# Gathers of routed rows that wait for the stores of the tiles in use: a Perceiver block with a routed expert layer on one core

## The chip, the core and the metric

The kernel runs on 1 core of a Trainium2 chip. The metric is the device time of one execution in microseconds (us). Before the change three runs gave 951.27, 951.43 and 955.66 us, so the median is 951.43 us.

## What is computed

The input is x (16 x 64 x 512, so 1024 tokens of 512 numbers) and a context of 16 x 1601 x 512. Three blocks follow one another: cross attention to the context, attention with relative positions, and a feed-forward block, each fed by a layer norm and added to its input. The last part of the feed-forward block is the mixture of experts that the change is about, cut here to what matters:

```python
def moe(xn, ...):
    xt = xn.reshape(B * S, H)                                   # 1024 tokens x 512
    shared = silu(xt @ Wg_s) * (xt @ Wu_s) @ Wd_s
    probs = sigmoid(xt @ W_router + routing_bias)               # 7 experts
    scores, idx = top_k(probs, 2)                               # 2 picks for each token
    scores = scores / sum(scores)
    ...
    hmid = silu(g) * u                                          # each expert: 512 -> 512, gate and up
    combined = einsum('tei,eih,te->th', hmid, Wd_r, wts)        # down, weighted by the scores
    return shared + combined
```

All matrices are float32. The routing comes from the data. With the inputs of the reference the 2048 picks fall on the seven experts as 358, 321, 268, 382, 193, 246 and 280.

## The kernel before, in words

Each engine has its own program, written out by hand, and waits on semaphores. TensorE multiplies, VectorE (DVE) and ScalarE (ACT) empty its banks and form the operands, GpSimd (POOL) forms low parts of weights and issues the indirect DMAs, and SyncE (SP) issues the loads and the stores of the result.

Every large product is made of three: a float32 operand is split into a high and a low part (names with `_hi` and `_lo`), and TensorE adds low x high, high x low and high x high.

**Slots and tiles.** A pick is a pair of token and expert. The picks are sorted by expert into slots, and each expert's slots are rounded up to whole tiles of 128 rows. However the picks fall, `TILES` = 2048 / 128 + 6 = 22 tiles are enough, and 22 are always computed. With the counts above the experts take 3, 3, 3, 3, 2, 2 and 3 tiles, that is 19 in all, numbered 0 to 18. The tiles 19 to 21 hold no pick; they are computed with the weights of the last expert. DVE works out slots, tiles and gates in `allot()`: `first` is the number of tiles ahead of each expert, and its last entry (column `NR` = 7) is the number of tiles in use.

**Two scratch tensors in HBM.** `x_slots` and `y_slots` have 22 x 128 rows of 512 numbers. SP fills `x_slots` with zeros early (L427), from an SBUF tile `zeros`. When the slots are known, POOL scatters the tokens' rows into `x_slots` with 16 indirect DMAs (L1159, 8 groups of tokens x 2 picks). Then the tile loop runs.

**The tile loop.** For tile t, ACT loads 128 rows of `x_slots` (L1464); TensorE transposes them (L968); DVE splits them (L2088, L2093); TensorE makes gate and up (L958 to L960); ACT applies silu (L1468); DVE multiplies (L2100); TensorE transposes again (L991); ACT and DVE split (L1472, L2104); TensorE makes the down product (L958 to L960 again); ACT copies it out (L1478) and stores it to `y_slots` (L1480), counting on the semaphore `y_stored[0]` for even t and `y_stored[1]` for odd t. The down product of tile t comes after gate and up of tile t + 1, so the store of tile t is issued late in the step of tile t + 1.

**Weights.** Expert weights stand in a ring of three places of 24 KB per partition, at 0, 24 and 48 KB for the high parts (`ring_hi`) and at 72, 96 and 120 KB for the low parts. `PLACES = [0, 2, 1, 0, 2, 1, 0]` says which expert stands where; the last one stands in place 0. SP loads (L443) and POOL splits (L1171, L1173), the last splits long before the tile loop ends.

**The end.** After its splits POOL waits for all stores, and gathers the rows back:

```python
            for i in range(2):
                pool.wait_ge(y_stored[i], 16 * (TILES // 2))
```

Then come 16 indirect DMAs (L1180), one for each group k of 128 tokens and each of its 2 picks, into `picked[0]` to `picked[15]`. They count on five semaphores: groups 0 and 1, groups 2 and 3, groups 4 and 5, group 6, group 7. DVE, after its last tile instruction (L2104 of tile 21), adds them with their gates into `y`, two instructions for each group (L2123, L2124), and SP stores each group of `y` to the output (L448). The stretch of the program around it:

## Time and profile before

| | |
|---|---|
| median of three runs | 951.43 us |
| lowest and highest run | 951.27 and 955.66 us |
| span of the profiled execution, first to last instruction | 949.6 us |
| TensorE matmul busy in it | 844.9 us (89%) |
| DVE busy | 513.4 us (54%) |
| ACT busy | 308.5 us (32%) |
| GpSimd busy | 346.5 us (36%) |
| mean granted TensorE clock | 0.957 |

The profiled execution is known by its span; the time around that span is not in the trace. The median of the runs is 1.8 us above the span, and this difference is used to go from one to the other. Times below are counted from the span's start. Busy shares are averages over three blocks of different kinds; what happens after the tile loop is read from its own stretch.

### The profile page before, as it was taken

To read this page: it belongs to the slowest core of one execution; us is meant where nothing else is said; L and a number is where in the kernel's file an instruction comes from. 1 tells how busy PE (TensorE), PEld (TensorE's weight loads), DVE (VectorE), ACT (ScalarE), POOL (GpSimd) and SP (SyncE) were. 2 spreads that over 40 slices of the span, in tenths; PEclk is the share of its full clock that TensorE was granted. 3 is DMA by queue.
4 is the path that set the end of the run, shared out by engine and by line. 5 is a ranking of instruction groups with operands and counts; after the bars stand their busy time and mean duration, and the time that the engine had idled before them with its cause. 6 is when DMAs were issued, how large, how long until landed. Compare 5 with 4: busy or idle time off the path is not lost.

```text
span 949.6 us, 15932 instructions
## 1 busy us (share of the span) xinstructions
PE 844.9 (89%) x6032; PEld 624.6 (66%) x6049; DVE 513.4 (54%) x1110; ACT 308.5 (32%) x820; POOL 346.5 (36%) x172
## 2 busy tenths in 40 slices
PE   1899999998999998989889999799979999979950
PEld 1555555454587788868656766588858888868840
DVE  7766688566621255436757668854734343333304
ACT  2222333222503266621166567523301112111110
POOL 0000000002407235520053324632769999880015
PEclk9999999999979999999989999999989999999975
DMA  9757776555200210020640000030373555421027
GB/s 351 310 186 271 278 272 229 214 213 196 81 10 1 65 71 1 11 63 0 235 187 1 1 0 1 1 133 1 133 269 130 190 186 199 160 72 55 34 67 232
DMA packets 43865, 121.25 MB, mean 128 GB/s; under 512 B 3984, under 2 KB 8080, under 8 KB 37920
## 3 DMA queue, kind: packets, MB, share of 16 engines
q1 hardware_dynamic: 34912, 100.52, 28.6%
q10 hardware_dynamic: 6336, 11.54, 3.5%
q0 software_dynamic: 2560, 8.39, 2.7%
q8 instruction: 41, 0.67, 0.3%
q14 instruction: 16, 0.13, 0.0%
HBM read 102.05 MB, written 18.38 MB: 127 GB/s over the span
## 4 chain that ended last, share of the span: by engine, by line
PE 74%; DVE 8%; POOL 7%; DMA 5%; ACT 2%; issue 2%; SPq 0%; POOLq 0%; ACTq 0%; DVEq 0%
PE scores L474 10%; PE bank L501 8%; PE bank L958 6%; PE bank L960 6%; PE bank L959 6%; DMA nat<-in_ctx_keys 3%; PE bank L774 2%; POOL x_slots L1159 2%; PE bank L731 2%; PE bank L629 2%; PE bank L787 2%; PE bank L549 2%; PE bank L697 2%; DVE ctxT L1552 2%; PE bank L698 2%
## 5 line engine op out<-in xcount | busy, mean ns | idle before, releaser
L1552 DVE STREAM_TRANSPOSE ctxT<-nat 128x1024 f32<-128x1024 f32 (+3 forms) x120 | 120.7, 1067 | 6.2 <-DMA nat<-in_ctx_keys 6.0
L474 PE MATMUL scores<-ctxT,hn 32*64 32x384 f32 (+2 forms) x2048 | 93.4, 508 | 13.7 <-DVE ctxT L1552 13.6
L501 PE MATMUL bank<-nat,probT 128*64 128x512 f32 (+1 forms) x416 | 94.3, 598 | 0.0
L1052 POOL TENSOR_TENSOR wq_lo<-wq_raw,wq_hi 128x1024 fp32r<-128x1024 f32 x4 | 9.3, 2343 | 228.4 <-ACT wq_hi L1239 228.4
L474 PEld LDWEIGHTS scores<-ctxT,hn 32*64 32x64 f32 x2048 | 65.3, 133 | 38.2 <-issue 26.1
L1099 POOL TENSOR_TENSOR sp<-sp,s_inv 128x512 f32<-128x512 f32 x32 | 32.6, 1040 | 140.9 <-DVE s_inv L1857 140.9
L1173 POOL TENSOR_TENSOR ring_lo<-ring_raw,ring_hi 128x2048 fp32r<-128x2048 f32 x18 | 82.9, 4606 | 1.4
L958 PE MATMUL bank<-ring_hi,xg_lo 128*128 x176 | 73.3, 416 | 0.4 <-DVE y L2070 0.4
L960 PE MATMUL bank<-ring_hi,xg_hi 128*128 x176 | 69.6, 396 | 0.0
L959 PE MATMUL bank<-ring_lo,xg_hi 128*128 x176 | 69.3, 394 | 0.0
L1171 POOL TENSOR_TENSOR ring_hi<-ring_raw,cst 128x2048 fp32r<-128x2048 f32 x18 | 64.9, 3603 | 10.8 <-DMA ring_raw<-in_Wexp 10.8
L501 PEld LDWEIGHTS bank<-nat,probT 128*64 128x64 f32 (+1 forms) x416 | 28.0, 137 | 53.5 <-issue 53.4
L2104 DVE TENSOR_TENSOR rhm_lo<-bank,rhm_hi 128x512 fp32r<-128x512 f32 x22 | 15.2, 692 | 81.5 <-ACT rhm_hi L1472 81.5
L1390 ACT ACTIVATE sp<-bank,s_bias 128x128 f32<-128x128 f32 x128 | 45.0, 386 | 27.4 <-DVE s_bias L1852 27.4
L1478 ACT COPY hn<-bank 128x512 f32<-128x512 f32 x22 | 12.9, 586 | 117.4 <-PE bank L960 117.4
L1180 POOL DMA_INDIRECT picked<-y_slots,slots x16 | 16.4, 1026 | 73.6 <-DMA y_slots<-hn 69.1
L1206 ACT ACTIVATE prob<-scores,nmax 128x512 f32<-128x512 f32 x24 | 16.2, 683 | 76.9 <-DVE nmax L1547 76.9
L2088 DVE TENSOR_SCALAR xg_hi<-bank,vec 128x128 fp32r<-128x128 f32 x88 | 24.8, 344 | 30.1 <-PE bank L968 29.8
L1543 DVE TENSOR_REDUCE mx<-scores 128x2 f32<-128x832 f32 x8 | 8.2, 1025 | 56.1 <-PE scores L474 56.1
L960 PEld LDWEIGHTS bank<-ring_hi,xg_hi 128*128 128x128 f32 x176 | 33.4, 190 | 7.7
L958 PEld LDWEIGHTS bank<-ring_hi,xg_lo 128*128 128x128 f32 x176 | 33.7, 191 | 6.3 <-issue 0.7
L959 PEld LDWEIGHTS bank<-ring_lo,xg_hi 128*128 128x128 f32 x176 | 33.7, 191 | 5.9
(277 smaller groups left out, 2010.4 us busy)
## 6 DMA issues: line engine op xcount, KB each, us to landing
nat<-in_ctx_keys SPq DMA_DIRECT2D x46, 1024.0 KB, 7.5
ring_raw<-in_Wexp SPq DMA_DIRECT2D x21, 1024.0 KB, 9.2
x_slots<-zeros SPq DMA_DIRECT2D x1, 5632.0 KB, 26.2
hn<-x_slots ACTq DMA_DIRECT2D x22, 256.0 KB, 3.1
y_slots<-hn ACTq DMA_DIRECT2D x22, 256.0 KB, 2.1
w_raw<-in_Wexp SPq DMA_DIRECT2D x3, 1024.0 KB, 11.2
nat<-in_ctx_keys SPq DMA_DIRECT2D x16, 130.0 KB
wq_raw<-in_Wq SPq DMA_DIRECT2D x1, 2048.0 KB, 7.6
```

The lines of the kernel that those rows point to most:

```text
L474: last = nc.tensor.matmul(scores4[64 * b:64 * b + 64, i, 0:KEYS_IN[i]], q4[rows_i, j, 64 * b:64 * b + 64], ctxT[rows_i, b, j, 0:KEYS_IN[i] ...
L501: last = nc.tensor.matmul(bank[7][64 * b:64 * b + 64, :], probT[0:n, j, 64 * b:64 * b + 64], nat[k % 2][0:n, b, j, :], start=j == 0, stop= ...
L549: nc.tensor.matmul(bank[4 + m % 4][:], lo, hh, start=c == 0, stop=False)
L958: nc.tensor.matmul(b[:], x_lo[:, c, :], hi, start=c == 0, stop=False)
L959: nc.tensor.matmul(b[:], x_hi[:, c, :], lo, start=False, stop=False)
L960: last = nc.tensor.matmul(b[:], x_hi[:, c, :], hi, start=False, stop=c == HC - 1)
L1099: nc.gpsimd.tensor_tensor(sp_[par][:, 4 * c:4 * c + 4, :], sp_[par][:, 4 * c:4 * c + 4, :], s_inv[par][:, 4 * c:4 * c + 4].unsqueeze(2).br ...
L1171: nc.gpsimd.tensor_tensor(ring_hi[at], ring_raw[at], zero, ALU.add).then_inc(split_hi, 1)
L1173: last = nc.gpsimd.tensor_tensor(ring_lo[at], ring_raw[at], ring_hi.bitcast(F32)[at], ALU.subtract)
L1390: last = nc.scalar.activation(sp_[par][:, h, :], score_bank(k, c)[:, n * P:(n + 1) * P], ACT.Exp, bias=s_bias[par][:, h:h + 1], scale=SELF ...
L1552: dve.transpose(dst, src).then_inc(columns_ready, 1)
L2088: last = dve.tensor_scalar(xg_hi[par][:, c, :], columns[c], weights[c], None, ALU.mult)
```

## The change

POOL no longer waits for all 22 stores before it gathers, but for the number of stores of each parity that the tiles in use make. DVE works these two numbers out with three small instructions in `allot()` (compare the tile numbers with the count of tiles in use, times 16, and add up even and odd tiles), and signals them on `slots_ready` as the fifth count. POOL reads them into registers after its splits, waits for `y_stored[0]` and `y_stored[1]` to reach them, passes a semaphore of its own (`used_stored`), and gathers. It waits for all 22 stores at its end.

`picked` moves from 0 to 32 KB to 24 to 56 KB per partition, that is out of the weight place 0 and into the places 1 and 2. SP fills `y_slots` with zeros too, in a second DMA right behind the first (22 x 128 rows, 5632 KB each), and POOL and DVE wait for both fills where they waited for one.

```diff
--- before.py
+++ after.py
@@ -160,7 +160,9 @@
         gates = [sbuf(ctx, f"gates{i}", [P, NT]) for i in range(2)]
         slots = sbuf(ctx, "slots", [P, NT, 2], U32)
         tile_expert = sbuf(ctx, "tile_expert", [P, 2, TILES], I32)
+        used_stored = sem("used_stored")
         expert_begins = sbuf(ctx, "expert_begins", [P, NE], I32)
+        stored_need = sbuf(ctx, "stored_need", [P, 2], I32)
         rbias_sb = sbuf(ctx, "rbias_sb", [P, NR])
         wrout_sb = sbuf(ctx, "wrout_sb", [P, HC, NR])
         a_max, a_bias, a_sum, a_inv = ([sbuf(ctx, f"{n}{i}", [P, NH]) for i in range(2)]
@@ -269,6 +271,8 @@
         r_fill = place(68, "r_fill", [P, NE, NE])
         r_tile = place(68.25, "r_tile", [P, 2, TILES])
         r_slot = place(68.5, "r_slot", [P, NT, 2])
+        r_used = place(68.75, "r_used", [P, TILES])
+        r_need = place(69, "r_need", [P, 2])
 
         ring_hi = place(0, "ring_hi", [P, RING3, 3, HC, D], F32R)
         ring_raw = place(72, "ring_raw", [P, RING3, 3, HC, D])
@@ -280,7 +284,7 @@
         rhm_hi = place(174, "rhm_hi", [P, HC, P], F32R)
         rhm_lo = place(148, "rhm_lo", [P, HC, P], F32R)
         yo = hn[2:4]
-        picked = [place(2 * i, f"picked{i}", [P, D]) for i in range(2 * NT)]
+        picked = [place(24 + 2 * i, f"picked{i}", [P, D]) for i in range(2 * NT)]
 
         pos_dram = nc.dram_tensor("pos_dram", (BATCH, SEQ * PADDED * NH), F32).ap()
 
@@ -424,8 +428,9 @@
                 sp.dma_start(w_raw[m][:], matrix(m, 0)).then_inc(raw_loaded, 16)
 
             sp.wait_ge(cleared, 3)
-            sp.dma_start(x_slots.rearrange("(t p) d -> p t d", p=P),
-                         zeros[:].unsqueeze(1).broadcast_to([P, TILES, D])).then_inc(slots_zeroed, 16)
+            for rows_of in (x_slots, y_slots):
+                sp.dma_start(rows_of.rearrange("(t p) d -> p t d", p=P),
+                             zeros[:].unsqueeze(1).broadcast_to([P, TILES, D])).then_inc(slots_zeroed, 16)
 
             for e in range(NR):
                 if e == 0:
@@ -1152,7 +1157,7 @@
                     columns_low(2 + 2 * j)
                     columns_low(3 + 2 * j)
 
-            pool.wait_ge(slots_zeroed, 16)
+            pool.wait_ge(slots_zeroed, 2 * 16)
             pool.wait_ge(slots_ready, 1)
             for k in range(NT):
                 for i in range(2):
@@ -1173,12 +1178,19 @@
                     last = nc.gpsimd.tensor_tensor(ring_lo[at], ring_raw[at], ring_hi.bitcast(F32)[at], ALU.subtract)
                 last.then_inc(split_ready, 1)
 
+            pool.wait_ge(slots_ready, 5)
+            need = [pool.value_load(stored_need[0:1, i:i + 1], min_val=16 * (TOK // P), max_val=16 * (TILES // 2))
+                    for i in range(2)]
             for i in range(2):
-                pool.wait_ge(y_stored[i], 16 * (TILES // 2))
+                pool.wait_ge(y_stored[i], need[i])
+            pool.sem_inc(used_stored, 1)
+            pool.wait_ge(used_stored, 1)
             for k in range(NT):
                 for i in range(2):
                     nc.gpsimd.indirect_dma_start(picked[2 * k + i][:], None, y_slots,
                                                  bass.IndirectOffsetOnAxis(slots[:, k, i:i + 1], 0)).then_inc(picked_loaded[picked_part(k)[0]], 16)
+            for i in range(2):
+                pool.wait_ge(y_stored[i], 16 * (TILES // 2))
 
         def query_out(copy, f, sem_done):
             copy(q4[:, 4 * f:4 * f + 4, :].rearrange("p j q -> p (j q)"), bank[QUERY_BANK[f]][:]).then_inc(sem_done, 1)
@@ -2035,7 +2047,10 @@
                 chain(dve.reciprocal(r_key[:], r_key[:]))
                 chain.mark(dve.tensor_tensor(gates[0][:], gates[0][:], r_key[:], ALU.mult))
                 dve.tensor_tensor(gates[1][:], gates[1][:], r_key[:], ALU.mult).then_inc(slots_ready, 1)
-                dve.wait_ge(slots_ready, 4)
+                chain(dve.tensor_scalar(r_used[:], cst[:, C_TILE:C_TILE + TILES], first[:, NR:NE], 16.0, ALU.is_lt, ALU.mult))
+                chain(dve.tensor_reduce(r_need[:], r_used[:].rearrange("p (t a) -> p a t", a=2), AX, ALU.add))
+                dve.tensor_copy(stored_need[:], r_need[:]).then_inc(slots_ready, 1)
+                dve.wait_ge(slots_ready, 5)
                 chain.wait()
 
             expert_stats(NT - 1, NT)
@@ -2045,7 +2060,7 @@
             expert_scale(NT // 2, NT)
             dve.tensor_copy(below_bf[:], cst[:, C_BELOW:C_BELOW + P]).then_inc(consts_cast, 1)
             dve.memset(ones_bf[:], 1.0).then_inc(consts_cast, 1)
-            dve.wait_ge(slots_zeroed, 16)
+            dve.wait_ge(slots_zeroed, 2 * 16)
             for j in range(NJ):
                 dve.wait_ge(silu_ready, j + 1)
                 if j >= 2:
```

Below are rows of the programs as they are built, in the order in which each engine issues them.

On POOL, the end of its program, before. The rows are the last two splits and the gathers; DMA stands for an indirect DMA:

```order
L1171 TENSOR_TENSOR ring_hi<-ring_raw,cst 128x2048 [waits routed_loaded2]
L1173 TENSOR_TENSOR ring_lo<-ring_raw,ring_hi 128x2048 [waits split_hi]
L1180 DMA picked0<-y_slots,slots 128x512 [waits y_stored1,y_stored0]
L1180 DMA picked1<-y_slots,slots 128x512
...
L1180 DMA picked15<-y_slots,slots 128x512
L122 UNCONDITIONAL_BRANCH
```

The same place after:

```order
L1176 TENSOR_TENSOR ring_hi<-ring_raw,cst 128x2048 [waits routed_loaded2]
L1178 TENSOR_TENSOR ring_lo<-ring_raw,ring_hi 128x2048 [waits split_hi]
L1182 TENSOR_LOAD stored_need [waits slots_ready]
L1182 ISA x2
L1182 TENSOR_LOAD stored_need
L1182 ISA x2
L1190 DMA picked0<-y_slots,slots 128x512 [waits y_stored0,y_stored1,used_stored]
L1190 DMA picked1<-y_slots,slots 128x512
...
L1190 DMA picked15<-y_slots,slots 128x512
L122 UNCONDITIONAL_BRANCH [waits y_stored1,y_stored0]
```

Two register loads have come between the splits and the first gather, the gathers stand in the same order, and the wait for all stores has gone behind the last of them.

On SP, the place where the scratch is filled, before (the four loads ahead of it are weights; L443 is the first load into the ring):

```order
L424 DMA w_raw32<-in_Wexp 128x4x512
L427 DMA x_slots<-zeros 128x22x512 [waits cleared]
L443 DMA ring_raw<-in_Wexp 128x4x512 [waits wo_full]
```

And after:

```order
L428 DMA w_raw32<-in_Wexp 128x4x512
L432 DMA x_slots<-zeros 128x22x512 [waits cleared]
L432 DMA y_slots<-zeros 128x22x512
L448 DMA ring_raw<-in_Wexp 128x4x512 [waits wo_full]
```

The second fill stands behind the first and ahead of the ring's loads; it waits for nothing of its own.

On DVE, the end of `allot()` and the shared expert's next step after the change (`gates` are the scores, `hm` the shared expert's hidden values):

```order
L2048 TENSOR_TENSOR gates0<-gates0,r_key 128x8 [waits dve_step]
L2049 TENSOR_TENSOR gates1<-gates1,r_key 128x8
L2050 TENSOR_SCALAR r_used<-cst,r_first 128x22
L2051 TENSOR_REDUCE r_need<-r_used 128x2 [waits dve_step]
L2052 CAST stored_need<-r_need 128x2 [waits dve_step]
L2068 TENSOR_TENSOR hm0<-act_g0,bank5 128x512 [waits silu_ready,hlo_ready,dve_step,slots_ready]
```

Three small instructions have come in ahead of that step. The rest of DVE's program, and TensorE's and ACT's, keep their order.

## Rows read from the trace of the kernel before

**Rows 1.** The page's first line.
```profile
span 949.6 us, 15932 instructions
```

**Rows 2.** Waits, 890 to 950 us: total us, times, longest us.
```profile
DVE y L2123 <- DMA picked<-y_slots,slots: 23.1, 5, 15.7
```

**Rows 3.** Timeline, ACT's queue: start us, us, line, operation.
```profile
892.75 0.36 ACTq L1480 DMA_DIRECT2D y_slots<-hn  x1
...
917.37 0.34 ACTq L1480 DMA_DIRECT2D y_slots<-hn  x1
```

**Rows 4.** Timeline, POOL, at the gathers.
```profile
920.25 0.98 POOL L1180 DMA_INDIRECT picked<-y_slots,slots  x1 [69.05 <-DMA y_slots<-hn]
...
927.80 1.39 POOL L1180 DMA_INDIRECT picked<-y_slots,slots  x1 [0.30 <-issue]
...
940.02 1.21 POOL L1180 DMA_INDIRECT picked<-y_slots,slots  x1 [0.30 <-issue]
```

**Rows 5.** Timeline, DVE, its last tile instruction and the additions.
```profile
911.27 0.69 DVE L2104 TENSOR_TENSOR rhm_lo<-bank,rhm_hi 128x512 fp32r<-128x512 f32 x1 [3.66 <-ACT rhm_hi L1472]
927.62 0.75 DVE L2123 SCALAR_TENSOR_TENSOR y<-picked,gates,y 128x512 f32<-128x512 f32 x1 [15.65 <-DMA picked<-y_slots,slots]
...
929.07 0.75 DVE L2123 SCALAR_TENSOR_TENSOR y<-picked,gates,y 128x512 f32<-128x512 f32 x1
...
934.64 0.77 DVE L2123 SCALAR_TENSOR_TENSOR y<-picked,gates,y 128x512 f32<-128x512 f32 x1 [4.03 <-DMA picked<-y_slots,slots]
...
942.59 0.75 DVE L2123 SCALAR_TENSOR_TENSOR y<-picked,gates,y 128x512 f32<-128x512 f32 x1 [0.73 <-DMA picked<-y_slots,slots]
...
945.57 0.75 DVE L2123 SCALAR_TENSOR_TENSOR y<-picked,gates,y 128x512 f32<-128x512 f32 x1 [1.44 <-DMA picked<-y_slots,slots]
946.36 0.75 DVE L2124 SCALAR_TENSOR_TENSOR y<-picked,gates,y 128x512 f32<-128x512 f32 x1
```

**Rows 6.** Timeline, DVE, first and last split of rows for the last expert.
```profile
851.30 1.12 DVE L2093 SCALAR_TENSOR_TENSOR xg_lo<-bank,vec,xg_hi 128x128 fp32r<-128x128 f32 x4 [7.99 <-POOL ring_lo L1173]
...
896.69 1.13 DVE L2093 SCALAR_TENSOR_TENSOR xg_lo<-bank,vec,xg_hi 128x128 fp32r<-128x128 f32 x4
```

**Rows 7.** The chain that ended last, in order of time.
```profile
917.37 2.05 DMA y_slots<-hn
919.46 0.79 issue
```

**Rows 8.** The page's DMA issues: count, KB each, median us to landing.
```profile
x_slots<-zeros SPq DMA_DIRECT2D x1, 5632.0 KB, 26.2
```

**Rows 9.** Timeline, SP's queue, around the fill.
```profile
460.74 2.77 SPq L427 DMA_DIRECT2D x_slots<-zeros  x1
624.01 197.79 SPq L443 DMA_DIRECT2D ring_raw<-in_Wexp  x21
```

**Rows 10.** Timeline, DVE, the shared expert's hidden values and the end of `allot()`.
```profile
631.40 0.63 DVE L2053 TENSOR_TENSOR hm<-act_g,bank 128x512 f32<-128x512 f32 x1
...
669.18 0.16 DVE L2037 TENSOR_TENSOR gates<-gates,r_key 128x8 f32<-128x8 f32 x1
...
673.97 0.69 DVE L2053 TENSOR_TENSOR hm<-act_g,bank 128x512 f32<-128x512 f32 x1 [2.53 <-ACT act_g L1448]
```

**Rows 11.** DMA queues, 900 to 950 us: packets, MB, share of 16 engines.
```profile
q0 software_dynamic: 1280, 4.20, 29.6%
q1 hardware_dynamic: 1152, 2.10, 11.0%
```

**Rows 12.** Timeline at the scatters, a DVE instruction and the scatter beside it.
```profile
682.19 2.28 DVE L2077 TENSOR_TENSOR ring_lo<-ring_raw,ring_hi 128x2048 fp32r<-128x2048 f32 x1
...
682.81 2.49 POOL L1159 DMA_INDIRECT x_slots<-xx,slots  x1 [0.30 <-issue]
```

**Rows 13.** Windows: us, then busy us (count) by engine, TensorE clock, DMA share, GB/s.
```profile
460.70:487.00 26.30, 21.70 (x100) 15.04 (x101) 20.32 (x74) 15.48 (x49) 4.24 (x5) 0.91 0.98 372
487.00:513.00 26.00, 25.52 (x178) 18.59 (x182) 16.21 (x34) 14.69 (x54) 14.06 (x7) 0.96 0.01 2
```

## The prediction

> **What bounds the kernel now.** I read the waits of the last 60 us first, then the timelines of the four engines that take part there, then the chain that ended last. The last multiplication feeds the store of tile 21, which ACT issues at 917.37 [rows 3]. It lands 2.05 us later and POOL starts 0.79 us after that [rows 7], at 920.25, after 69.05 us without work [rows 4]. POOL then issues 16 gathers one after another, the last one at 940.02, some 1.3 us apiece. DVE had finished its tile work at 911.27 + 0.69 = 911.96 and stood idle for 15.65 us; after that it waited three more times in the rows shown, the last until 945.57, and ended at 946.36 + 0.75 = 947.11 [rows 5]. In all DVE waited 23.1 us for gathered rows [rows 2]. So from 917 to 947 us nothing but the gathers sets the time: the end is their start plus 26.9 us, and the span ends 2.5 us after DVE, at 949.6 [rows 1], with the last output store.
>
> **Which tiles are in use.** The change pays only if the last tile in use is earlier than tile 21. The routing counts of the inputs give 19 tiles, the last one number 18. The trace bears out where the last expert begins: at 851.30 DVE waited 7.99 us for POOL's last split, the one wait on a new expert's weights so late. The last such step, at 896.69, is that of tile 21 [rows 6]; between the two lie four more steps, so 851.30 is tile 16, and the expert's 280 picks fill tiles 16, 17 and 18. There are two stores between the two of [rows 3] (tiles 19 and 20), so the one at 892.75 is that of tile 18. Even tiles 0 to 18 are 10 stores and odd tiles 1 to 17 are 9.
>
> **The gathers' new start.** The store of tile 18 is issued at 892.75. With the same landing and start as for tile 21, POOL begins at 892.75 + 2.05 + 0.79 = 895.6, which is 24.7 us earlier. The register loads of the two counts stand before the wait, and POOL is idle for 69 us there [rows 4], so they are hidden by about 40 us. The semaphore that POOL raises and waits for itself isn't in the trace; between nothing and the 0.30 us that POOL leaves between two gathers I take 0.1 and leave it out of the sum, since what follows does not hang on it.
>
> **What DVE does then.** It can't use the rows before 911.96, its last tile instruction, which comes from TensorE and has nothing to do with the gathers. By the old distances the rows of groups 0 and 1 are there at 927.62 - 24.7 = 903.0, those of 2 and 3 at 910.0, those of group 6 at 917.9 and of group 7 at 920.9 [rows 5]. DVE's additions come in pairs 929.07 - 927.62 = 1.45 us apart, and a pair takes 947.11 - 945.57 = 1.54. Starting at 912.0 it comes to group 6 at 920.7 and to group 7 at 922.1, behind the rows by 2.7 and 1.2 us. So it adds without a pause and ends at 912.0 + 7 x 1.45 + 1.54 = 923.7. Before it ended at 947.1: **23.4 us less**. The gathers' wait is gone, and what is late next is DVE itself, by a narrow 1.2 us over the last gather. TensorE's last product (before 917) and tile 21's store (landing at 919.4) end earlier than that, so POOL's wait for all stores at its end costs nothing. The output stores leave as DVE ends each group, 1.45 us apart; eight of them are 11.0% of 50 us, 0.7 us of all 16 engines each [rows 11], so they keep up and the last 2.5 us stay.
>
> **The second fill.** The first one goes out at 460.74 and lands 26.2 us later, at 487 [rows 8, 9]. It used the DMA engines wholly (share 0.98); in the next 26 us they are all but idle, 0.01 [rows 13]. The second fill takes those, to 513. SP's next load goes out at 624.01 [rows 9], and DVE's first instruction behind the fill's wait is at 631.40 [rows 10]. That is a cover of 111 us; without it the cost would be 26.2. The weights' loads stand ahead of the fills in the queue. What other work there is at 487 to 513 can be slowed only by traffic that it doesn't issue itself. As a bound: TensorE was busy 21.7 of 26.3 us in the first fill and 25.5 of 26.0 after it [rows 13]. If all of that were the fill's doing, the second would cost up to 3.8 us. Self-attention is just starting in the first window, with one step's work and no neighbour to fill in, so I take 0.
>
> **DVE's three small instructions.** They are like the small ones beside them, 0.16 us each and a little for the step's semaphore, 0.2 apiece [rows 10]: 0.6 us, and they delay the hidden values that follow at once. The next of these waits 2.53 us for ACT, until 673.97 [rows 10], so the delay is swallowed there. The scatters are released earlier, by the slots, and don't see it. 0 on the path, 0.6 if that slack were gone. The place of `picked` changes nothing that is timed: places 1 and 2 have no reader once tile 15 is done, place 0 still has.
>
> **Sum.** 23.4 less than the span of 949.6 is 926.2; the median of the runs stands 1.8 above the span, which gives **928.0 us**.
>
> **A rule weighed against the trace.** At 927.80 a gather that began beside DVE's addition took 1.39 us, against 0.98 for the first one [rows 4], and at 682.81 a scatter beside a DVE instruction of 2.28 us, both of whose inputs are in SBUF, took 2.49 [rows 12]; that one was stopped for all of it. The four last gathers now fall between 911 and 917 and so beside unbroken additions. The Trainium skill, "SBUF — State Buffer", Who interferes with whom, says that a DVE instruction with two SBUF inputs contends with a GpSimd instruction that reads SBUF, and that the loser is blocked for the whole instruction. By the scatter's row each of the four would be held for a whole addition, 0.75 us: 3.0 us, while 0.6 of such delay is in the old times already (1.39 - 0.98, and 1.21 - 0.98 in the last one) [rows 4]; group 7 would then be there at 920.9 + 3.0 - 0.6 = 923.3, 1.2 us after DVE comes to it, and the time would be 929.2. By the gather's own row, 0.4 each, group 7 is there at 920.9 + 1.6 - 0.6 = 921.9, before DVE comes to it at 922.1, and the sum stands. I take the gather's row.
>
> **Rivals.**
> 1. The gathers stay the bound. They now run beside tile work, tile stores and output stores. For it: the slack is only 1.2 us, and the sixteen gathers are 29.6% of 50 us, 0.9 us of all engines each [rows 11], at one in 1.3 us; with an output store of 0.7 in every 1.45 us that is more than 1. Against: only four or five gathers meet output stores, and in the old run ten did. Price, at the worst row for every gather (1.39 + 0.30): the last starts 15 x 1.69 = 25.4 after 895.6, at 921.0, lands 5.55 later (940.02 to 945.57), at 926.5; then 1.54 and 2.5 and 1.8: 932.4. It decides from 1.2 us of delay on.
> 2. The second fill slows self-attention by the 3.8 us above: 931.8.
> 3. The wait is not shortened, because the count of tiles in use comes out as 22: no gain, and up to 0.6 us of small instructions, 951.4 to 952.0. The last expert's start at tile 16 speaks against it.
> 4. The other side, slower: something on the path at 487 to 513 waits until the second fill has drained. If it stood still for the fill's whole 26.2 us, the time would be 928.0 + 26.2 = 954.2, slower than before by 2.8; the point from which it decides the sign is a stop of 23.4 us, and it takes 28.2, more than the fill is long, to be slower by over half a per cent. In the first fill, just as dense, DVE was busy for 20.3 of 26.3 us [rows 13], so nothing stood still.
>
> **How the numbers follow.** Forecast as reasoned 0.74, between 926 and 929.5; rival 1 0.12, 929 to 932.4; rival 2 0.05; rival 3 0.03; rival 4 0.02 (mostly with its time a little under the bound of half a per cent); something unthought that eats between 5 and 20 us of the gain 0.04. The range is 925.5 to 932.5: the low end is the DVE-bound end less what three runs can differ (lowest and highest before are 4.4 apart, so 2.5), since no gather can bring the end before DVE's 923.7; the high end takes in rivals 1 and 2. About 0.87 lies inside. Half a per cent, 4.8 us, is about what a measurement can tell from no change: faster 0.95, same 0.035, slower 0.015.
>
> **What would show each step.** In the changed kernel's timeline the first gather should start at 895 to 896, about 2.8 us after the fourth-last tile store. DVE should start adding within 0.1 us of its last tile instruction and have no wait for gathered rows, or under 0.5 us at groups 6 and 7. SP should issue two fills by 466, the second landing near 513, with TensorE's busy time in 487 to 513 as now. The tile loop should end where it did, at 912 for DVE and 917 for TensorE. The prediction is wrong if DVE waits for the last groups by more than 2 us, if the tile loop starts later than before, or if the first gather still follows tile 21.

## The result, and the profile after

The changed kernel took 938.09 us (median of four runs, 932.90 to 938.98), the kernel before 951.35 us (the three runs already told and a fourth, 949.93 to 955.66): a ratio of 0.9839, interval 0.9807 to 0.9872. It is faster, by 1.6%, but the time lies 10.1 us above the forecast of 928.0 and 5.6 us above the top of the range. The profiled execution took 932.9 us and had a span of 931.0, 5.0 to 6.2 us less than the spans of the other three; it alone has a trace. The page's first line:

```profile
span 931.0 us, 15960 instructions
```

The first gathers do what was predicted. ACT's queue and ACT (the store of tile 18, the silu of tile 21's gate, the copy of tile 20's down product), in the timeline of the changed kernel:

```profile
888.14 0.36 ACTq L1492 DMA_DIRECT2D y_slots<-hn  x1
...
908.08 0.60 ACT L1480 ACTIVATE rhm<-bank 128x512 f32<-128x512 f32 x1 [10.08 <-remote]
...
913.90 0.59 ACT L1490 COPY hn<-bank 128x512 f32<-128x512 f32 x1 [5.22 <-remote]
```

POOL in the same timeline, its first and its last gather:

```profile
891.09 0.98 POOL L1190 DMA_INDIRECT picked<-y_slots,slots  x1 [44.12 <-POOLq L1186]
...
909.90 0.95 POOL L1190 DMA_INDIRECT picked<-y_slots,slots  x1 [0.30 <-issue]
```

The first gather starts 2.95 us after the store of tile 18; the prediction had 2.84. Both come about 4.6 us earlier than [rows 3] let expect, since in this execution the whole tile loop ran that much earlier, well before any gather (set 2 below shows where that comes from). DVE in the same timeline, from its multiplication of tile 20 on:

```profile
893.68 0.69 DVE L2115 TENSOR_TENSOR rhm<-rhm,bank 128x512 f32<-128x512 f32 x1 [0.45 <-PE bank L965]
...
898.04 0.69 DVE L2119 TENSOR_TENSOR rhm_lo<-bank,rhm_hi 128x512 fp32r<-128x512 f32 x1 [3.67 <-issue]
913.78 0.69 DVE L2115 TENSOR_TENSOR rhm<-rhm,bank 128x512 f32<-128x512 f32 x1 [15.05 <-remote]
916.29 0.69 DVE L2119 TENSOR_TENSOR rhm_lo<-bank,rhm_hi 128x512 fp32r<-128x512 f32 x1 [1.83 <-ACT rhm_hi L1484]
916.90 0.74 DVE L2138 SCALAR_TENSOR_TENSOR y<-picked,gates,y 128x512 f32<-128x512 f32 x1
...
927.04 0.75 DVE L2138 SCALAR_TENSOR_TENSOR y<-picked,gates,y 128x512 f32<-128x512 f32 x1
```

The waits for gathered rows of [rows 2] and [rows 5] are gone: DVE adds without a pause, 10.14 us from the first pair to the last, and starts 0.08 us before its last tile instruction ends (916.29 + 0.69 = 916.98), so right behind it. A new wait of 15.05 us stands ahead of tile 21's multiplication. It needs the product "up" of tile 21, and the releaser is given as "remote": no engine's instruction in the trace ended there. The views of the waits (890 to 950 us) and of TensorE's timeline say what had been done by then. The waits:

```profile
DVE rhm L2115 <- remote: 15.0, 1, 15.0
ACT rhm L1480 <- remote: 10.1, 1, 10.1
```

TensorE, the last matmul of the gate of tile 21, of its up, of the down of tile 20, and then its next work:

```profile
899.19 0.39 PE L965 MATMUL bank<-ring_hi,xg_hi 128*128 x1
...
901.91 0.39 PE L965 MATMUL bank<-ring_hi,xg_hi 128*128 x1
...
904.63 0.39 PE L965 MATMUL bank<-ring_hi,rhm_hi 128*128 x1
914.52 1.11 PE L996 MATMUL bank<-cst,rhm 128*128 128x128 f32 x4 [9.51 <-DVE rhm L2115]
```

TensorE ended the gate at 899.58, the up at 902.30 and the down at 905.02. ACT took the gate at 908.08, DVE the up at 913.78, ACT the down at 913.90: 8.5, 11.5 and 8.9 us after the last matmul of each. In `e1_again` below, DVE starts within 0.1 us of the same product's end. So the work was finished and the word of it came late. The gathers are in the air just then: the last is issued by 910.85, and the last record of a landing of theirs is at 913.71. The trace's semaphore records show the rise itself as late (908.06, 913.75 and 913.88). Only TensorE's word is late: ACT's silu ends at 908.68, and DVE's wait for it (L2114) is over at 908.74, as the chain that ended last has it:

```profile
908.72 0.02 DVEq L2114
908.74 5.02 another core or an unknown queue
913.75 0.02 issue
913.78 0.70 DVE rhm L2115
```

The trace also has 379 records of semaphore rises fewer than that of the kernel before (5034 against 5413; `e1_again` below, the same kernel, has 5431), missing at the scatters (671 to 690 us) and at the gathers (896 to 908). I call this **the stop** below.

The window that holds it, with the columns of [rows 13]:

```profile
893.00:917.40 24.40, 13.41 (x60) 10.59 (x59) 3.41 (x6) 2.94 (x5) 13.58 (x15) 0.79 0.63 192
```

TensorE is busy for 13.4 of 24.4 us. Its mean granted clock is 0.79 there, but that is no cause: the last matmuls before the stop are 0.23 us apart, as those of the other profiles are, and the clock is 1.00 from 893 to 905 us and 0.61 from 905 to 914.5, so it fell once the engine had nothing to do.

The fills (SP's queue, and the landing of the second), and the window after the first fill:

```profile
462.21 2.63 SPq L432 DMA_DIRECT2D x_slots<-zeros  x1
464.88 16.09 SPq L432 DMA_DIRECT2D y_slots<-zeros  x1
...
625.45 1.48 SPq L448 DMA_DIRECT2D ring_raw<-in_Wexp  x3
```

```profile
y_slots<-zeros SPq DMA_DIRECT2D x1, 5632.0 KB, 38.5
```

```profile
487.00:513.00 26.00, 25.71 (x158) 19.46 (x157) 15.37 (x33) 15.37 (x50) 15.55 (x9) 0.93 0.57 222
```

SP was held 16.09 us by the issue of the second fill, against 2.63 by the first, yet its next load leaves at 625.45, against 624.01 before [rows 9]. The second fill lands 38.5 us after its issue, at 503.4, about 14 us behind the first and not 26. TensorE is busy for 25.71 of 26.00 us in the window in which it runs, against 25.52 before [rows 13].

### The profile page after: what moved, and what is told of

Its sections match the earlier page's. It is cut to its first block, busy times and chain, and to the rows that moved or that the text cites. A ratio compares the mean times of both kernels' runs of the same rounds, so it can differ in the third digit from the quotient of the medians.

```text
span 931.0 us, 15960 instructions
## 1 busy us (share of the span) xinstructions
PE 847.3 (91%) x6048; PEld 624.6 (67%) x6049; DVE 512.5 (55%) x1113; ACT 308.4 (33%) x820; POOL 341.8 (37%) x172
## 4 chain that ended last, share of the span: by engine, by line
PE 73%; DVE 8%; POOL 8%; DMA 5%; issue 3%; ACT 2%; another core or an unknown queue 1%; SPq 0%; POOLq 0%; DVEq 0%; ACTq 0%
PE scores L479 10%; PE bank L506 8%; PE bank L963 4%; PE bank L965 4%; PE bank L964 4%; DMA nat<-in_ctx_keys 3%; POOL ring_lo L1178 3%; PE bank L779 2%; POOL ring_hi L1176 2%; PE bank L736 2%; PE bank L792 2%; PE bank L554 2%; PE bank L634 2%; PE bank L702 2%; DVE ctxT L1564 2%
## 5 line engine op out<-in xcount | busy, mean ns | idle before, releaser
L479 PE MATMUL scores<-ctxT,hn 32*64 32x385 f32 (+2 forms) x2048 | 94.9, 512 | 13.3 <-DVE ctxT L1564 13.2
L479 PEld LDWEIGHTS scores<-ctxT,hn 32*64 32x64 f32 x2048 | 65.8, 134 | 38.6 <-issue 27.5
L1555 DVE TENSOR_REDUCE mx<-scores 128x2 f32<-128x832 f32 x8 | 8.2, 1024 | 56.3 <-PE scores L479 56.3
L2103 DVE TENSOR_SCALAR xg_hi<-bank,vec 128x128 fp32r<-128x128 f32 x88 | 24.8, 345 | 24.7 <-PE bank L973 24.4
L963 PE MATMUL bank<-ring_hi,rhm_lo 128*128 x88 | 35.1, 399 | 1.5 <-DVE rhm_lo L2119 1.5
## 6 DMA issues: line engine op xcount, KB each, us to landing
y_slots<-zeros SPq DMA_DIRECT2D x1, 5632.0 KB, 38.5
```

The costliest lines, as they stand in the source:

```text
L479: last = nc.tensor.matmul(scores4[64 * b:64 * b + 64, i, 0:KEYS_IN[i]], q4[rows_i, j, 64 * b:64 * b + 64], ctxT[rows_i, b, j, 0:KEYS_IN[i] ...
L963: nc.tensor.matmul(b[:], x_lo[:, c, :], hi, start=c == 0, stop=False)
L2103: last = dve.tensor_scalar(xg_hi[par][:, c, :], columns[c], weights[c], None, ALU.mult)
```

## The experiments

A set is a group of kernels run one after the other on one chip, together with the kernel before; ratios are to the kernel before of the same set. The result above is set 1; sets 2 to 9 follow, 8 on the chip of 7 and 9 on that of 5. "The stop" is the late word from TensorE in the profile above.

**Set 2: the changed kernel again, and with single parts changed.** `e1_again` is the changed kernel as it is.

> The changed kernel once more. In its first profile the gates product of tile 21 ended on TensorE near 899 us, but its semaphore reached ScalarE at 908.06, and that of the up product reached VectorE at 913.75 instead of near 902; 915 us is also about where the last gathered rows landed. Theory G (the gathers hold something back that TensorE's signals or the engines' code need): the same stop of 9 to 15 us in tile 20 or 21 is seen again, ending near the landing of the last gather, and the span is 930 to 938. Theory L (a single mishap of one execution): no stop, VectorE's last tile instruction ends at 912 and the span is 926 to 927.

929.42 us (927.87 to 931.96), ratio 0.9782 (0.9723 to 0.9840), span 927.4. The stop isn't there. DVE in its timeline:

```profile
899.52 0.69 DVE L2115 TENSOR_TENSOR rhm<-rhm,bank 128x512 f32<-128x512 f32 x1 [0.45 <-PE bank L965]
...
908.18 0.69 DVE L2115 TENSOR_TENSOR rhm<-rhm,bank 128x512 f32<-128x512 f32 x1 [3.61 <-PE bank L965]
912.52 0.69 DVE L2119 TENSOR_TENSOR rhm_lo<-bank,rhm_hi 128x512 fp32r<-128x512 f32 x1 [3.65 <-ACT rhm_hi L1484]
913.12 0.74 DVE L2138 SCALAR_TENSOR_TENSOR y<-picked,gates,y 128x512 f32<-128x512 f32 x1
...
923.27 0.75 DVE L2138 SCALAR_TENSOR_TENSOR y<-picked,gates,y 128x512 f32<-128x512 f32 x1
924.05 0.75 DVE L2139 SCALAR_TENSOR_TENSOR y<-picked,gates,y 128x512 f32<-128x512 f32 x1
```

And POOL, the first gather and the last three:

```profile
896.93 0.98 POOL L1190 DMA_INDIRECT picked<-y_slots,slots  x1 [44.26 <-POOLq L1186]
...
913.24 1.45 POOL L1190 DMA_INDIRECT picked<-y_slots,slots  x1 [0.30 <-issue]
914.99 1.14 POOL L1190 DMA_INDIRECT picked<-y_slots,slots  x1 [0.30 <-issue]
916.44 1.15 POOL L1190 DMA_INDIRECT picked<-y_slots,slots  x1 [0.30 <-issue]
```

This sizes the stop. From the multiplication of tile 20 to the last split it is 912.52 - 899.52 = 13.00 us here and 916.29 - 893.68 = 22.61 in set 1: **9.6 us late**. From the split to group 7 it is 10.75 us in both.

The profiled execution of set 1 isn't 9.6 us longer than this one, though, but 3.6 (spans of 931.0 and 927.4), since its tile 20 came 5.8 us earlier (893.68 against 899.52). The like late signals at POOL's scatters go with that. DVE in set 1's timeline, an addition of the shared expert and its next two long splits of weights, and POOL, the scatter that was held longest and the last one:

```profile
682.34 0.69 DVE L2085 TENSOR_TENSOR y<-bank,y 128x512 f32<-128x512 f32 x1 [4.06 <-remote]
682.94 2.28 DVE L2092 TENSOR_TENSOR ring_lo<-ring_raw,ring_hi 128x2048 fp32r<-128x2048 f32 x1
...
689.28 2.28 DVE L2092 TENSOR_TENSOR ring_lo<-ring_raw,ring_hi 128x2048 fp32r<-128x2048 f32 x1
```

```profile
684.16 1.90 POOL L1164 DMA_INDIRECT x_slots<-xx,slots  x1 [0.30 <-issue]
...
688.89 0.96 POOL L1164 DMA_INDIRECT x_slots<-xx,slots  x1 [0.30 <-issue]
```

And POOL in `e1_again`, the last of the three scatters that were held there and the last of all:

```profile
687.25 2.50 POOL L1164 DMA_INDIRECT x_slots<-xx,slots  x1 [0.31 <-issue]
...
692.58 0.96 POOL L1164 DMA_INDIRECT x_slots<-xx,slots  x1 [0.30 <-issue]
```

The scatters begin at 668.8 and 668.9 us. In `e1_again`, as in [rows 12], three of them stand beside DVE's splits and take 2.4 to 2.5 us each; in set 1 DVE came late, one scatter was held, and the last ended 3.7 us earlier. The store of tile 0 was issued at 715.9 us there, against 722.2. So in the traced execution the stop cost 9.6 us at tile 21, and late signals at the scatters had given most of 5.8 us ahead of it. The median of set 1 less 9.6 is 928.5, close to this set's 929.42, but the two belong to different executions: 938 is the time of three that have no trace. It would fit if they had the late tile 21 without the early tile loop (927.4 + 9.6 = 937.0, an estimate, against spans of 936.0 to 937.2); that is not shown.

`e2_late` keeps everything but the early start:

```diff
                 pool.wait_ge(y_stored[i], need[i])
+            for i in range(2):
+                pool.wait_ge(y_stored[i], 16 * (TILES // 2))
             pool.sem_inc(used_stored, 1)
```

> All of the change but the early start: POOL waits for the counts of the tiles in use and then for all 22 stores before it gathers. It keeps the second fill, the three small instructions, the register loads and the new place of the gathered rows. If the prediction's zeros for these hold, 951.4 us, within 1. If the second fill or the small instructions are what is missing from the gain, 955 to 962, with the loss seen before 893 us. The stop in tile 21 should be gone in every theory in which early gathers cause it.

953.76 us (ten runs, 949.05 to 955.35), ratio 1.0034 (1.0006 to 1.0063); the profiled execution had a span of 949.6, the same as before's. The median is 2.4 us above the 951.4 expected. So the second fill, the small instructions, the new place and the register loads give back at most 0.6%, and the profile shows none of it. The early start, all that parts this kernel from `e1_again`, is worth 953.76 - 929.42 = 24.3 us.

`e3_place96` puts the gathered rows in a third place:

```diff
-        picked = [place(24 + 2 * i, f"picked{i}", [P, D]) for i in range(2 * NT)]
+        picked = [place(96 + 2 * i, f"picked{i}", [P, D]) for i in range(2 * NT)]
```

> The change with the gathered rows at 96 to 128 KB of each partition instead of 24 to 56 KB. If the stop comes from where the gathers write (near the weights at 0 to 24 KB that TensorE reads), it goes or moves and the time is 928. If it comes from the gathers as such, the time is that of the changed kernel, 933 to 939, and the stop is there.

927.09 us, ratio 0.9748 (0.9683 to 0.9813). No stop in it, but none in the kernel beside it either, so it says only that this place costs nothing.

`e4_plain_sp` drops POOL's gathers; SP copies as many bytes with plain DMAs, the first 2048 rows of the scratch instead of the routed ones, so the routed gather is left out:

```diff
+            sp.wait_ge(used_stored, 1)
+            for k in range(NT):
+                for i in range(2):
+                    sp.dma_start(picked[2 * k + i][:], y_slots[(2 * k + i) * P:(2 * k + i + 1) * P, :]).then_inc(
+                        picked_loaded[picked_part(k)[0]], 16)
...
-                    nc.gpsimd.indirect_dma_start(picked[2 * k + i][:], None, y_slots,
-                                                 bass.IndirectOffsetOnAxis(slots[:, k, i:i + 1], 0)).then_inc(picked_loaded[picked_part(k)[0]], 16)
```

> The change with the 16 gathers replaced by 16 plain DMAs of the same size from SyncE, started by the same counts of stores; they copy rows 0 to 2047 of the scratch and not the routed rows, so the output differs. If the stop comes from indirect DMAs that GpSimd issues, it is gone: VectorE ends its tile work at 912, adds without a pause, and the time is 928. If the load on the DMA engines itself does it, the stop stays, maybe shorter, since plain loads of 256 KB take about 2 us each: 930 to 936.

928.65 us, ratio 0.9774 (0.9710 to 0.9838). SP's queue issued all sixteen by 903.7:

```profile
895.12 8.61 SPq L454 DMA_DIRECT2D picked<-y_slots  x16
```

DVE added from 912.07, a pair every 1.45 us as in `e1_again`. Faster transfers win nothing: DVE is the bound, not the gathers.

**Set 3: load, order and the other bound.** `e5_again` is the changed kernel once more.

> The changed kernel a third time. Theory L (the stop in tile 21 that the first profile showed is a rare event, or belongs to one chip): no stop in the profile, 925.5 to 932.5 us, and a ratio of 0.975 to 0.98. Theory G (the gathers cause it each time with some chance): among six executions at least one is 5 us or more above the fastest, and the profile shows the stop again with a chance of one half.

928.87 us (six runs, 925.54 to 931.15), ratio 0.9767 (0.9736 to 0.9798), no stop. `e6_double` puts 16 more gathers, thrown away, ahead of the real ones:

```diff
+            for i in range(2):
+                pool.wait_ge(y_stored[i], 16 * 8)
+            for k in range(NT):
+                for i in range(2):
+                    nc.gpsimd.indirect_dma_start(picked[2 * k + i][:], None, x_slots,
+                                                 bass.IndirectOffsetOnAxis(slots[:, k, i:i + 1], 0)).then_inc(scattered, 16)
+            pool.wait_ge(scattered, 16 * 4 * NT)
```

> The change with 16 more gathers of the same size, thrown away, that begin when the stores of tiles 0 to 15 have landed (near 867 us) and end ahead of the true ones, so that three more tiles are computed beside gathers. If gathers hold back TensorE's signals (theory G), stops of 5 us or more now show in tiles 17 to 21 too, and the time is 933 or more. If they don't (theory L), the tile loop keeps its 9.1 us for each tile and the time is 926 to 931; the added gathers are hidden, since they end by about 891, before the store of tile 18 lands.

927.73 us, ratio 0.9764 (0.9731 to 0.9798). POOL's first gather of each kind:

```profile
868.03 0.98 POOL L1188 DMA_INDIRECT picked<-x_slots,slots  x1 [16.48 <-DMA y_slots<-hn]
...
895.30 0.94 POOL L1197 DMA_INDIRECT picked<-y_slots,slots  x1 [7.53 <-POOLq L1193]
```

32 gathers beside the tile loop delay no tile, in a set whose unchanged kernel has no stop either. So gathers do not slow the loop by their number or their traffic alone; what stopped set 1 takes something more.

`e7_between` lets DVE add groups 0 and 1 before the last tile's multiplication:

```diff
+            add_rows(range(2))
             routed_mult(TILES - 1)
             hidden_split(TILES - 1)
...
+            add_rows(range(2, NT))
```

> The change with VectorE's additions for groups 0 and 1 moved into its idle time of 3.6 us between its last instructions for tile 20 and tile 21. The end of the changed kernel is set by 8 pairs of additions behind tile 21; two of them, 2 x 1.45 = 2.9 us, now lie in idle time if their rows are there at 904, as they should be (7.4 us after the first gather). If VectorE's additions set the end, 2.9 us less than the changed kernel of the same call. If the gathers do, no change, and VectorE waits for the last groups.

927.09 us, ratio 0.9748 (0.9718 to 0.9778). DVE now waits for the rows of group 0 and for those of group 7:

```profile
906.09 0.75 DVE L2137 SCALAR_TENSOR_TENSOR y<-picked,gates,y 128x512 f32<-128x512 f32 x1 [1.06 <-DMA picked<-y_slots,slots]
...
922.62 0.75 DVE L2137 SCALAR_TENSOR_TENSOR y<-picked,gates,y 128x512 f32<-128x512 f32 x1 [1.65 <-DMA picked<-y_slots,slots]
```

Its first gather started at 897.38, so group 7's rows were there 25.2 us after it. In `e1_again` that would be 922.1, and DVE came to them at 923.27: a slack of 1.1 us, against the 1.2 predicted. Taking 2.9 us of additions off DVE's end can therefore win only 1.1 to 1.8 us, and the two medians differ by 1.8 with intervals that overlap.

`e8_tile20` starts the gathers one even tile later, after tile 20's store:

```diff
                 pool.wait_ge(y_stored[i], need[i])
+            pool.wait_ge(y_stored[0], 16 * 11)
             pool.sem_inc(used_stored, 1)
```

> The change, but the gathers also wait for the store of tile 20, the first after tile 18 of the even ones. They then start 2.8 us after 910.3, at 913.1, and the last rows land 25.3 us later at 938.4, or 22.6 us later as in the first profile of the changed kernel, at 935.7; with 1.5 for the last pair, 2.5 to the span's end and 1.8 around it the time is 941.5 to 944.2. So 13 to 16 us of the gain come from the two last tiles, and the first of the three would be worth little, since VectorE is the bound from there on. If the start of the gathers mattered one for one, it would be 17.5 us over the changed kernel, 945 to 947.

944.67 us (941.97 to 944.98), ratio 0.9929 (0.9900 to 0.9957). POOL, its first gather:

```profile
914.53 0.98 POOL L1191 DMA_INDIRECT picked<-y_slots,slots  x1 [61.41 <-POOLq L1187]
```

DVE, the first addition and that of group 7:

```profile
922.44 0.75 DVE L2139 SCALAR_TENSOR_TENSOR y<-picked,gates,y 128x512 f32<-128x512 f32 x1 [9.21 <-DMA picked<-y_slots,slots]
...
939.02 0.75 DVE L2139 SCALAR_TENSOR_TENSOR y<-picked,gates,y 128x512 f32<-128x512 f32 x1 [0.42 <-DMA picked<-y_slots,slots]
```

Here the gathers bound the end again. They start 17.6 us later than in `e1_again`, and the additions of group 7 are 15.8 us later (939.02 - 923.27): between the two lie 1.8 us of slack, by this reading. The time is 0.5 us over what was expected at most; the gathers started at 914.53 where 913.1 had been reckoned.

**Sets 4 to 6: to meet the stop again.** Set 4 is `e9_again` (the changed kernel) and `e10_plain_sp` (as `e4_plain_sp`):

> The changed kernel a fourth time, to see whether the stop before tile 21's last steps comes back. In the first set all four executions stood at 933 to 939; in two later sets ten stood at 925.5 to 932.0, without a stop in either profile. Theory C (it belongs to the chip of that set): on another chip again 926 to 932 without a stop. Theory G (chance, from the gathers): a stop in the profile, or single executions at 933 or more.

> Plain DMAs of SyncE in place of the gathers once more (rows 0 to 2047 of the scratch, so the output differs), beside the changed kernel. If the changed kernel of this call shows the stop and this one doesn't, indirect DMAs from GpSimd cause it; if both show it, the load of the DMA engines does; if neither does, both are 926 to 931 and nothing is told but that the stop is rare.

928.63 us, ratio 0.9763 (0.9732 to 0.9794), and 929.17 us, ratio 0.9783 (0.9756 to 0.9811). No stop in either. Set 5 is `e11_again`:

> The changed kernel in a fifth set. Theory C (the stop belongs to the chip or the moment of the first set): no stop, 926 to 932, unless the set falls on that chip, where all executions would stand at 933 to 939 again. Theory G (the gathers bring it by chance): a stop in the profile or single executions at 933 or more.

929.31 us, ratio 0.9775 (0.9740 to 0.9810), no stop. Set 6 is `e12_aftermult`, which moves the additions of groups 0 and 1 one step on from where `e7_between` has them:

```diff
             routed_mult(TILES - 1)
+            add_rows(range(2))
             hidden_split(TILES - 1)
...
+            add_rows(range(2, NT))
```

> As the kernel with two groups' additions ahead of tile 21's last steps, but they stand one step later, between VectorE's multiplication and its split of tile 21, where it has 3.65 us without work (908.87 to 912.52 in the repeated run of the changed kernel). In the earlier version VectorE waited for group 0 until 906.1 and tile 21's multiplication came 0.5 us late; here the rows are there and nothing is late, and the two pairs fill 2.9 us. The last group's rows then set the end: 25.2 us after the first gather, against 26.3 us in the changed kernel, so about 1.1 us less than that: 927.5 to 928, within what can be told from the changed kernel. If the additions were still the bound, it would be 2.9 less.

932.12 us (930.33 to 935.02), ratio 0.9866 (0.9841 to 0.9891), with the kernel before at 944.76 in that set. **The stop is back.** Its waits (890 to 950 us):

```profile
DVE rhm L2115 <- remote: 15.4, 1, 15.4
ACT rhm L1480 <- remote: 13.9, 1, 13.9
```

And ACT and DVE in its timeline:

```profile
911.87 0.60 ACT L1480 ACTIVATE rhm<-bank 128x512 f32<-128x512 f32 x1 [13.91 <-remote]
914.07 0.69 DVE L2115 TENSOR_TENSOR rhm<-rhm,bank 128x512 f32<-128x512 f32 x1 [15.38 <-remote]
```

The tile before was at 893.64, as in set 1. The gate product ended at 899.5 and ACT saw it 12.3 us later; the up product ended at 902.3, and DVE saw it 11.8 us later. Again records of semaphore rises are missing at the scatters and at the gathers (5016 are there). As in set 1 only one scatter was held (2.03 us), and the store of tile 0 went out at 716.2. Ratios tell the two cases apart as the traces do: 0.9839 and 0.9866 with the stop, 0.9736 to 0.9787 for the unchanged code without it. The time alone hardly does, 932.1 us against 927.6 to 930.1, because the kernel before was faster too, 944.76 against 950.2 to 952.3 in the other sets from 2 on; late signals at its scatters, with nothing to delay at its end, would do that, but no trace of it was kept in this set. The additions that this kernel moves stand behind the late multiplication, so they haven't made it late; by its trace up to there this is the changed kernel, in a set that has the stop.

**Sets 7 to 9: the chip, or the indirect DMAs?** Set 7 is `e13_plain_sp` (as `e4_plain_sp`):

> Plain DMAs of SyncE in place of the 16 gathers (rows 0 to 2047 of the scratch, so the output differs). The two profiles with the stop also show TensorE's signals 6 us late beside GpSimd's scatters near 682 us, which this kernel keeps. So each set tells by the scatters whether it is of the kind that shows the stop. Theory I (indirect DMAs issued by GpSimd hold TensorE's signals back on some chips): in such a set the scatters show late signals, and tile 21 doesn't, VectorE ends its tile work at its usual time. Theory D (any dense load of the DMA engines does it there): tile 21 shows late signals of 5 us or more as well. In a set without late signals at the scatters both say 926 to 931 and nothing is told.

928.08 us, ratio 0.9744 (0.9712 to 0.9776). DVE in its timeline, an addition of the shared expert while POOL's scatters run, and then tile 21:

```profile
681.46 0.69 DVE L2086 TENSOR_TENSOR y<-bank,y 128x512 f32<-128x512 f32 x1 [3.31 <-PE bank L1028]
...
908.32 0.69 DVE L2116 TENSOR_TENSOR rhm<-rhm,bank 128x512 f32<-128x512 f32 x1 [3.60 <-PE bank L970]
```

At the scatters TensorE's signals come up to 2.9 us late in this execution (5.9 in set 1 and 6.2 in `e12_aftermult`, where the like of the 3.31 us wait shown is 4.1 and 4.2 us; it is 2.03 in the kernel before), and records are missing there again (5285 are there); at tile 21, beside plain DMAs, nothing is late: 3.60 us is the usual wait. Set 8, on the same chip, is `e14_plain_sp` and `e15_again`:

> Plain DMAs in place of the gathers again (other rows, so the output differs), beside the changed kernel on the same chip. In a set whose scatters show late signals of TensorE: theory I, no late signal in tile 21 here, 925 to 930 us, and 4 to 10 us less than the changed kernel. Theory D, the stop here too and the same time. In a set without them both kernels are within 2 us.

> The changed kernel beside e14. In a set whose scatters show late signals: the stop in tile 21 and 932 to 939 us, a gain of 13 to 18 us instead of 22. In a set without them: 926 to 932, no stop.

926.77 us, ratio 0.9721 (0.9690 to 0.9753), and 927.57 us, ratio 0.9736 (0.9701 to 0.9772). No late signal in either, at scatters or gathers: the chip alone doesn't decide. Set 9, on the chip of set 5, is `e16_again`, `e17_between` and `e18_plain_sp`:

> The changed kernel with the next two on one chip. e13 and e14 were the same kernel on the same chip, one with late signals at the scatters and one without, so it is not the chip as such. If it belongs to a stretch of time or to a program as loaded, about two of seven profiles of this kind show it: then 932 to 939 with the stop, otherwise 926 to 932.

> The kernel with two groups' additions ahead of tile 21's last steps, beside the changed kernel: 0.7 to 2 us less than e16 if neither shows the stop, since the last gathered rows are the bound at 25.2 us after the first gather. With the stop, VectorE is late anyway and the time is 930 or more.

> Plain DMAs in place of the gathers (other rows, so the output differs). Theory I: even if the scatters show late signals, tile 21 shows none and the time is 926 to 930. Theory D: with them, a stop of 5 us or more in tile 21.

930.09 us, ratio 0.9787 (0.9754 to 0.9820); 930.55 us, ratio 0.9773 (0.9735 to 0.9812); 927.11 us, ratio 0.9733 (0.9693 to 0.9772). No stop in any of the three. Adding two groups ahead of the last tile is not shown to beat the changed kernel on either chip, and the plain DMAs are 0.5% ahead here, with intervals that overlap, and level in the other sets.

## Why the prediction was right in its steps and wrong in its time

- **The gathers' new start: right.** 2.95 us after the store of tile 18 in set 1 and in `e1_again`, 2.84 predicted; the difference is the 0.1 us set aside for the semaphore. In [rows 4] the like start was 27.5 us after that same store.
- **DVE the next bound, by a narrow margin: right.** In `e1_again` DVE adds from 913.12 in pairs of 1.45 us and ends at 924.80; predicted 912.0, 1.45 and 923.7. The 1.1 us between are the tile loop's, which ended that much later in this execution. The slack over group 7 is 1.1 us by `e7_between` and 1.8 by `e8_tile20`, predicted 1.2. The rule that was weighed went as taken: the gathers that met additions in `e1_again` took 0.2 to 0.5 us more and not 0.75, and DVE did not wait for group 7. `e4_plain_sp` shows that no faster transfer would help, `e8_tile20` what the kernel is when they do bound it. Rival 1 (the gathers stay the bound) falls with that.
- **The second fill at nothing: right as far as the runs tell.** TensorE's busy time beside it is that of before, DVE and SP are covered as said, and `e2_late` has before's span. Its runs stand above the kernel before by an interval of 0.06 to 0.63%, so rival 2's 3.8 us (0.4%) isn't excluded by the times; the profile speaks against it. Its length was wrong: the prediction gave it the first fill's 26.2 us, to 513, and it was over at 503.4; the first one's time also holds the weights' loads ahead of it in the queue (four of 1024 KB in the window from 460 us). SP's queue was held for 16.09 us, which the prediction had not reckoned, and 144 us without work behind it hid that.
- **The small instructions at nothing: right.** They took 0.9 us rather than 0.6 and shortened the wait behind them, from 2.53 [rows 10] to 1.8 us.
- **"The tile loop should end where it did": this step failed.** The prediction took the tile loop's last tile as a thing that "has nothing to do with the gathers", put DVE's start at 912.0 from it, and had no term and no rival for what the gathers would do to TensorE's side of it. In set 1's traced execution TensorE's finished products were made known 8.5 to 11.5 us late while the gathers ran, and the last tile ended 9.6 us late, reckoned from tile 20: DVE began to add at 916.90 instead of 912.0, although tile 20 had been early. The three executions that set the median lie 5 to 6 us higher still, with no trace to tell it apart. The cause stays open. Before the change the gathers began when no product was awaited, so the same thing would have cost nothing there. The case "something unthought that eats between 5 and 20 us" was this one; it had 0.04.
- **Where the stop is absent, the whole number held.** The unchanged code, timed in six more sets, took 927.57, 928.63, 928.87, 929.31, 929.42 and 930.09 us: each within 2.1 us of 928.0 and inside the range.

What is shown of the stop and what not: it was met with POOL's indirect gathers in two of the twelve profiles in which they run beside the last tiles; it was met at POOL's scatters in the same two and, weaker, in `e13_plain_sp`; in the five profiles in which plain DMAs took the gathers' part, one of them with the late signals at its scatters, tile 21 was never late. It seems to stay with a set (the three further executions of set 1, by their times of 937.8 to 939.0, had it too), changes from set to set on one chip, and isn't brought by twice as many gathers. That the indirect DMAs delay TensorE's signals fits all of this, but it rests on coincidence in three profiles; no experiment could turn it on. Another coincidence points the same way: in set 1 the last late rises come as the landings end, at the gathers (last landing recorded at 913.71, rises at 913.75 and 913.88) and at the scatters (691.61; 691.56 and 691.69). What makes one set have it and another not stays open, and so does whether the missing records are its cause, its effect or only the trace's loss: every timed run here was recorded like the profiled ones, so none tells whether the recording itself takes part.

## What to carry to other kernels

When a wait is shortened so that a transfer runs beside the end of another stage, that stage's end becomes a term of the sum: look for what the transfer shares with it, and give a case of its own to the stage ending late. When a narrow slack is what follows, the next bound lies just behind it; here a further 2.9 us taken off DVE would win at most 1.8. And time such a kernel in more than one set: one set here gave 938, six others 928 to 930, and the interval of the one (0.9807 to 0.9872) holds none of the others' ratios (0.9736 to 0.9787). And follow an oddity back to every place where it occurs: here it lengthened one stage and shortened another.

## What the runs showed of the hardware that was not expected

**Late signals.** A finished matmul group was seen by ACT and DVE 8.5 to 12.3 us after its end in two profiles, within 0.1 us being the usual, while GpSimd's indirect DMAs were running; TensorE itself went on through its queue meanwhile, and in set 1 ACT's signal to DVE took under 0.1 us in the midst of it.

**A gather beside DVE's additions was held for less than one of them.** The last three gathers of `e1_again` took 1.45, 1.14 and 1.15 us against 0.95 for one beside no addition: 0.3 us more on the mean, 0.5 at most, beside additions of 0.75. The Trainium skill, "SBUF — State Buffer", Who interferes with whom, says that a DVE instruction with two SBUF inputs contends with a GpSimd instruction that reads SBUF, and that the loser is blocked while the other's instruction lasts. This trace agrees that the two contend; the shorter hold doesn't speak against the rest, since a gather can meet an addition that is part done, and the trace doesn't tell which it met. The scatters beside the long splits agree in size: 2.4 to 2.5 us in `e1_again` beside an instruction of 2.28.

**A DMA's issue can hold its queue.** The second fill of 5632 KB, issued behind another of that size, kept SP's queue for 16.09 us (15.35 in `e1_again`), the first for 2.6 to 2.9 us.
